# A graph layer on one core: who adds the mask, who finds the row maxima, and who issues which DMA in the edge stage

## The chip, the cores and the metric

The kernel runs on one core of a Trainium2 chip. The metric is the device time of one execution in microseconds (us); the figure before the change is the median of three runs.

## What is computed

The reference has two graph layers behind a layer norm and a ReLU each, with a residual sum. The change touches the second one only:

```python
def _L1_gnn_ref(x, adj, weight, bias, node_w, edge_w):
    node_att = jax.nn.softmax(x @ node_w, axis=0)
    h = x @ edge_w
    e = h @ h.T
    e = jnp.where(adj > 0, e, NEG_BIG)
    edge_att = jax.nn.softmax(e, axis=1)
    combined_att = node_att * edge_att
    support = x @ weight
    output = adj * combined_att @ support
    return output + bias
...
h = jnp.maximum(_layernorm(x, axis=-1), 0.0)
x = x + _L1_gnn_ref(h, adj, ...)
```

There are N = 3327 nodes and 256 features, in f32; `NEG_BIG` is -9e15. The row softmax needs the maximum of each row of the masked 3327 x 3327 scores before the exponential.

## The kernel before

The program has four parts: the first layer (two steps, from the start to about 3400 us of the span), `phase_mid` (layer norm, `h`, `support`), and `phase_edges`, the stage of the change, which runs from 3650 us to the end. `phase_edges` takes the rows in `NT` = 26 blocks of 128. Per block t, in the order in which the data goes:

- SyncE's queue loads 128 rows of the adjacency into `adj` (3 slots, 1664 KB, line 1155 and 1161) and 128 x 256 of the residual into `xr` (2 slots, lines 1157 and 1165). In the loop of lines 1158 to 1165 it waits for `w_ready` of t, loads block t+3, then waits for `out_ready` of t, stores the result of t (line 1163), and loads `xr` of t+2.
- VectorE, `penalty` (line 1210): 0 or NEG_BIG in bf16, `pen`, from `adj`.
- TensorE, `scores` (lines 1289 and 1290): 7 chunks (six of 512 columns, one of 255), in 2 PSUM banks by turns. A chunk takes six f16 matmuls (`hth`, `htl` are the high and low halves of `h`) and a seventh one of `identb` with `pen`, which adds the mask in PSUM. Chunk n waits until chunk n-2 has been taken (`lg_free`), and the first chunk of a block for `pen_ready`.
- VectorE, `take` (line 1218): copies a chunk to `em` (3 slots) and finds its row maxima with the same instruction, into `mx`; `highest` (line 1223) reduces the 7 maxima to `nb`.
- ScalarE, `exponent` (line 1186): exp over the row with its sum.
- GpSimd (line 1180): `em` times `adj`, 128 x 3328 (`w_ready`). It may start only behind the exponential.
- TensorE, `transposes` (line 1299), 26 blocks of 128 columns in 7 groups q; ScalarE copies each group to f16, `wh` (line 1200), and VectorE makes the low half `wl` (line 1265).
- TensorE, `attend` (lines 1310 to 1312): three matmuls of 256 columns for each of the 26.
- VectorE, `finish` (lines 1227 to 1237): reciprocal of the sum, residual plus bias (line 1229), factor times node attention (line 1231), and the output (line 1237), which goes to `o`.

The order on each engine is written out by hand, with scores running two blocks ahead (`AHEAD`). In block t TensorE does, for q = 0 to 6: transposes(t, q), scores(t+2, q), and from q = 2 on attend(t, q-2); then attend(t, 5) and attend(t, 6). VectorE does for each q: wl(t, q), take(t+2, q), and behind q = 2 finish(t-1); then highest(t+2) and penalty(t+3). ScalarE does for each q the copy, and behind q = 1 exponent(t+1). Every engine waits in its own order, so an instruction that waits holds all that stand behind it on its engine.

Of the kernel before, what the change touches and what calls it, by code (L numbers as in the profile page):

```python
# [15 lines left out]
P = 128  # L16
# [1102 lines left out]
def phase_edges(nc, sem_in, psum, sb_in, env):  # L1119
# [5 lines left out]
    with ExitStack() as c:  # L1125
# [5 lines left out]
        identb = sb("e_identb", [P, P], BF16)  # L1131
# [5 lines left out]
        mx = sb("e_mx", [P, 3, NCH], F32)  # L1137
# [7 lines left out]
            "ax_done", "fac_ready", "xr_ready", "out_ready", "zero", "identb", "pen_ready")}  # L1145
# [5 lines left out]
        @block.sync  # L1151
        def _(sp):
            sp.dma_start(bias[:], env["bias"]).then_inc(S["bias_in"], 16)
            for t in range(3):
                sp.dma_start(adj[:, t], adjR[t]).then_inc(adj_in[t], 16)
            for t in range(2):
                sp.dma_start(xr[:, t], x1_d[:, t, :]).then_inc(xr_in[t], 16)
            for t in range(NT):
                if t + 3 < NT:
                    sp.wait_ge(S["w_ready"], t + 1)  # L1160
                    sp.dma_start(adj[:, t % 3], adjR[t + 3]).then_inc(adj_in[t % 3], 16)
                sp.wait_ge(S["out_ready"], t + 1)
                sp.dma_start(out[:, t, :], o[:, t % 2]).then_inc(stored[t % 2], 16)  # L1163
                if t + 2 < NT:
                    sp.dma_start(xr[:, t % 2], x1_d[:, t + 2, :]).then_inc(xr_in[t % 2], 16)  # L1165
            for u in range(2):
                sp.wait_ge(stored[u], 16 * (NT // 2))

        @block.gpsimd
        def _(pool):  # L1170
# [6 lines left out]
            for t in range(NT):  # L1177
                pool.wait_ge(adj_in[t % 3], 16 * (t // 3 + 1))
                pool.wait_ge(S["exp_done"], t + 1)
                nc.gpsimd.tensor_tensor(em[:, t % 3], em[:, t % 3], adj[:, t % 3], ALU.mult).then_inc(S["w_ready"], 1)  # L1180

        @block.scalar
        def _(act):
# [6 lines left out]
            nc.scalar.activation(natt[:], natt[:], ACT.Exp, bias=col[:, 2:3], accum_out=col[:, 3:4]).then_inc(na["exps"], 1)  # L1190
            act.wait_ge(S["zero"], 1)
            exponent(0)
            for t in range(NT):
                for q in range(NGRP):
# [6 lines left out]
                    if q == 1 and t + 1 < NT:  # L1201
                        exponent(t + 1)

        @block.vector
        def _(dve):
            def penalty(t):
                dve.wait_ge(adj_in[t % 3], 16 * (t // 3 + 1))
                if t >= 2:
                    dve.wait_ge(S["lg_done"], NCH * (t - 1))
                nc.vector.tensor_scalar(pen[:, t % 2, 0:N], adj[:, t % 3, 0:N], 0.0, NEG_BIG, ALU.is_le, ALU.mult).then_inc(S["pen_ready"], 1)  # L1210

            def take(t, ch):
                n = NCH * t + ch
                w = chunk_width(ch)
                if ch == 0 and t >= 3:
                    dve.wait_ge(S["tr_done"], NGRP * (t - 2))
                dve.wait_ge(S["lg_done"], n + 1)
                nc.vector.tensor_scalar(em[:, t % 3, ch * CH:ch * CH + w], psL[n % 2][:, 0:w], 1.0, None, ALU.mult, ALU.max,  # L1218
                                        accum_out=mx[:, t % 3, ch:ch + 1]).then_inc(S["lg_free"], 1)

            def highest(t):
                dve.wait_ge(S["lg_free"], NCH * (t + 1))
                nc.vector.tensor_reduce(nb[:, t % 3:t % 3 + 1], mx[:, t % 3], AX.X, ALU.max, negate=True).then_inc(S["nb_ready"], 1)

            def finish(t):
                u = t % 2
                nc.vector.reciprocal(fac[:, u:u + 1], den[:, t % 3:t % 3 + 1]).then_inc(S["fac_ready"], 1)
                dve.wait_ge(xr_in[u], 16 * (t // 2 + 1))
                nc.vector.tensor_tensor(xr[:, u], xr[:, u], bias[:], ALU.add).then_inc(S["xr_ready"], 1)  # L1229
                dve.wait_ge(S["fac_ready"], 2 * t + 1)  # L1230
                nc.vector.tensor_tensor(fac[:, u:u + 1], fac[:, u:u + 1], natt[:, t:t + 1], ALU.mult).then_inc(S["fac_ready"], 1)
# [9 lines left out]
            nc.vector.tensor_copy(identb[:], ident[:]).then_inc(S["identb"], 1)  # L1241
            dve.wait_ge(S["bias_in"], 16)
# [34 lines left out]
        def _(pe):  # L1277
            def scores(t, ch):
# [3 lines left out]
                if ch == 0:  # L1282
                    pe.wait_ge(S["pen_ready"], t + 1)
# [3 lines left out]
                for i, (lhs, rhs) in enumerate(((hth, hth), (hth, htl), (htl, hth))):  # L1287
                    for k in range(KC):
                        nc.tensor.matmul(bank, lhs[:, k, rows], rhs[:, k, cols], start=(i + k == 0), stop=False)  # L1289
                nc.tensor.matmul(bank, identb[:], pen[:, t % 2, cols], start=False, stop=True).then_inc(S["lg_done"], 1)  # L1290
# [25 lines left out]
            pe.wait_ge(S["identb"], 1)  # L1316
# [49 lines left out]
```

## Time and profile before

| what | value |
|---|---|
| median of 3 runs | 4305.14 us (4302.59 to 4307.82) |
| the profiled execution: its time | 4310.23 us |
| the profiled execution: its span | 4308.4 us |
| mean granted TensorE clock over the span | 0.884 |
| PE busy / PEld busy | 3101.3 us (72%) / 2139.9 us (50%) |
| DVE busy | 3669.6 us (85%) |
| ACT busy | 2984.8 us (69%) |
| POOL busy | 321.9 us (7%) |

PE is TensorE's matmul side, PEld its weight loads, DVE is VectorE, ACT is ScalarE, POOL is GpSimd, SP is SyncE, and SPq and ACTq are the sides of SP and ACT that issue DMAs. The busy shares are means over stages with different limits, so they are read here by stage. In a timeline a row gives start, duration, engine, line, operation, and tiles (written <- read), then the count; what stands in brackets is the idle time before it and what ended it. Two matmuls in a row overlap in their durations, so the cost of a group is read from its start to the start of the next.

### The profile page before, as it was taken

The numbers are of one execution on the slowest core, as the hardware profiler recorded it, in microseconds if no ns is written. First come the engines' busy times: TensorE is split into PE (matmuls) and PEld (weight loads), VectorE is DVE, ScalarE is ACT, GpSimd is POOL, SyncE is SP. The second block draws the span as 40 slices with busy tenths as digits, with TensorE's granted clock in tenths as the row PEclk, the third lists the DMA queues.
The fourth block names the chain that finished last, engine by engine and source line by source line (L and its number), as shares of the span: only waits on it lengthen the run. The fifth ranks groups of instructions, "written<-read, shape, count | busy, mean of one in ns | idle before, by whom it ended". The sixth has DMA issues, their size and how long they took to land. (4 is left out here: it accounts for less than half of the span.)

```text
span 4308.4 us, 41843 instructions
## 1 busy us (share of the span) xinstructions
PE 3101.3 (72%) x14280; PEld 2139.9 (50%) x14330; DVE 3669.6 (85%) x4935; ACT 2984.8 (69%) x3947; POOL 321.9 (7%) x319
## 2 busy tenths in 40 slices
PE   2646787877878785558786877968777344988888
PEld 2335565665656664424353443534444233566666
DVE  3399999999999999599999999999999543666766
ACT  1299999999999971499999999899980111222222
POOL 0000000000000000000000000000000132322322
PEclk9968988988989997879898988989888667999999
DMA  0111212212212121311111111111111231122221
GB/s 34 42 52 56 90 49 73 76 63 82 69 61 82 57 81 52 125 33 41 46 32 37 41 36 42 32 37 43 36 43 31 82 97 64 67 91 74 74 92 45
DMA packets 108035, 254.24 MB, mean 59 GB/s; under 512 B 11888, under 2 KB 47792, under 8 KB 104368
## 3 DMA queue, kind: packets, MB, share of 16 engines
q1 hardware_dynamic: 89104, 224.32, 16.2%
q10 hardware_dynamic: 18720, 27.27, 1.7%
q8 instruction: 113, 1.85, 0.2%
q14 instruction: 98, 0.80, 0.1%
HBM read 217.47 MB, written 34.08 MB: 58 GB/s over the span
## 5 line engine op out<-in xcount | busy, mean ns | idle before, releaser
L619 DVE SCALAR_TENSOR_TENSOR s_dump<-s_rows,s_mid 128x3327 bf16<-128x3327 f32 x684 | 2518.1, 3681 | 0.7 <-issue 0.2
L569 ACT ACTIVATE s_adump<-s_rows,s_mid 128x3327 bf16<-128x3327 f32 (+1 forms) x304 | 933.6, 3071 | 9.9
L574 ACT ACTIVATE s_adump<-s_rows,s_mid 128x3327 bf16<-128x3327 f32 (+1 forms) x304 | 930.0, 3059 | 5.9 <-ACT s_sx_out L480 3.1
L767 PE MATMUL bank<-x,s_slab 128*128 128x512 f32 x1352 | 615.5, 608 | 0.0
L810 PE MATMUL bank<-hb,s_wT 128*128 128x256 f32 x1352 | 359.8, 411 | 121.1 <-ACT s_wT L458 120.9
L810 PE MATMUL bank<-xab,s_wT 128*128 128x256 f32 x1352 | 351.2, 404 | 114.9 <-ACT s_wT L458 114.9
L767 PEld LDWEIGHTS bank<-x,s_slab 128*128 128x128 f32 x1352 | 265.4, 197 | 314.9 <-issue 308.8
L1200 ACT ACTIVATE e_wh<-bank 128x512 f16<-128x512 f32 (+1 forms) x182 | 102.5, 565 | 448.2 <-PE bank L1299 448.1
L458 ACT ACTIVATE s_wT<-bank 128x512 f32<-128x512 f32 (+1 forms) x364 | 201.2, 553 | 287.5 <-PE bank L799 287.5
L799 PE MATMUL bank<-ident,s_rows 128*128 128x128 f32 x1352 | 227.7, 295 | 181.0 <-DVE s_rows L639 181.0
L746 PE MATMUL bank<-kh,qs 128*128 128x512 f16 (+1 forms) x364 | 145.4, 399 | 282.2 <-DVE s_rows L598 271.7
L810 PEld LDWEIGHTS bank<-hb,s_wT 128*128 128x128 f32 x1352 | 260.0, 203 | 171.8 <-ACT s_wT L458 81.5
L810 PEld LDWEIGHTS bank<-xab,s_wT 128*128 128x128 f32 x1352 | 257.6, 201 | 166.8 <-ACT s_wT L458 74.2
L767 PE MATMUL bank<-hb,s_slab 128*128 128x257 f32 x1352 | 340.2, 406 | 0.0
L799 PEld LDWEIGHTS bank<-ident,s_rows 128*128 128x128 f32 x1352 | 186.2, 156 | 244.8 <-DVE s_rows L639 189.2
L767 PEld LDWEIGHTS bank<-hb,s_slab 128*128 128x128 f32 x1352 | 278.8, 207 | 53.9 <-issue 4.8
L598 DVE TENSOR_SCALAR_CACHE_REDUCE s_rows<-bank 128x512 f32<-128x512 f32 (+1 forms) x364 | 233.1, 644 | 61.3 <-PE bank L747 59.2
L1180 POOL TENSOR_TENSOR e_rows<-e_rows,e_adj 128x3328 f32<-128x3328 f32 x26 | 187.9, 7226 | 429.1 <-ACT e_rows L1186 429.1
L746 PEld LDWEIGHTS bank<-kh,qs 128*128 128x128 f16 x364 | 38.1, 105 | 356.2 <-DVE s_rows L598 321.0
L1265 DVE TENSOR_TENSOR e_wl<-bank,e_wh 128x512 f16<-128x512 f32 (+1 forms) x182 | 117.8, 649 | 106.1 <-ACT e_wh L1200 106.1
L639 DVE SCALAR_TENSOR_TENSOR s_rows<-s_rows,s_mid 128x3327 f32<-128x3327 f32 x52 | 191.4, 3680 | 0.9
L1310 PE MATMUL bank<-sup,e_wh 128*128 128x256 f16 x676 | 185.1, 274 | 8.7 <-DVE e_wl L1265 7.4
(175 smaller groups left out, 4657.1 us busy)
## 6 DMA issues: line engine op xcount, KB each, us to landing
s_slab<-adjT_dram SPq DMA_DIRECT2D x104, 448.0 KB, 3.8
e_adj<-adjR_dram SPq DMA_DIRECT2D x26, 1664.0 KB, 7.4
s_slab<-adjT_dram SPq DMA_DIRECT2D x104, 384.0 KB, 3.6
strip<-adjR_dram SPq DMA_DIRECT2D x52, 448.0 KB, 3.5
strip<-adjR_dram SPq DMA_DIRECT2D x52, 384.0 KB, 3.3
su_d<-s_su_out ACTq DMA_DIRECT2D x26, 256.0 KB, 2.0
zu_d<-s_zu_out ACTq DMA_DIRECT2D x26, 256.0 KB, 2.0
sx_d<-s_sx_out ACTq DMA_DIRECT2D x26, 256.0 KB, 2.0
```

The lines of the kernel that those rows point to most:

```text
L458: nc.scalar.activation(wT[:, n % 2, 0:w], bank_of("quad", n)[:, 0:w], ACT.Copy).then_inc(S["ev_done"], 1)
L569: nc.scalar.activation(adump[:], row(g, 2), ACT.Sign, bias=st(mid, g, 2), accum_out=cnt[:]).then_inc(S["a_eval"], 1)
L574: nc.scalar.activation(adump[:], row(g, 2), ACT.Relu, bias=st(mid, g, 2), accum_out=gap[:]).then_inc(S["a_eval"], 1)
L598: nc.vector.tensor_scalar(rows[:, home(g, r), ch * CH:ch * CH + w], psL[n % 2][:, 0:w], 1.0, None, ALU.mult, ALU.max, accum_out=mx[:, home ...
L619: nc.vector.scalar_tensor_tensor(out=dump[:], in0=row(g, r), scalar=st(mid, g, r), in1=row(g, r), op0=ALU.is_gt, op1=ALU.mult, accum_out=s ...
L639: nc.vector.scalar_tensor_tensor(out=row(g, r), in0=row(g, r), scalar=st(mid, g, r), in1=row(g, r), op0=ALU.is_gt, op1=ALU.mult, accum_out ...
L746: nc.tensor.matmul(psL[n % 2][:, 0:w], lhs, kh2[:, cols], start=True, stop=False)
L767: ins = nc.tensor.matmul(acc, slab[:, i % NSLAB, j - PIECES[p], :], s_op[:, j, 0:SN], start=False, stop=(j == NT - 1))
L799: ins = nc.tensor.transpose(bank[:, k * P:(k + 1) * P], rows[:, home(g, r), j * P:(j + 1) * P], ident[:])
L810: ins = nc.tensor.matmul(psA[f % 2][:, 0:D], wT[:, n % 2, k * P:(k + 1) * P], a_op[:, j, 0:D], start=(j == 0), stop=(j == NT - 1))
L1180: nc.gpsimd.tensor_tensor(em[:, t % 3], em[:, t % 3], adj[:, t % 3], ALU.mult).then_inc(S["w_ready"], 1)
L1310: nc.tensor.matmul(acc, wh[:, n % 4, blk], sup[:, j, 0:D], start=(j == 0), stop=False)
```

## The change

The mask leaves TensorE: the seventh matmul of each chunk, with `identb`, is gone, and so is TensorE's wait for `pen_ready`. `take` becomes a sum of the bank and `pen` on VectorE without the maxima, and `highest` reduces the whole row of 3327 from `em`. The sum of residual and bias goes from VectorE's `finish` to GpSimd, behind the multiplication of the same block. Line 1231 becomes an instruction with a per-partition scalar in place of one with two tensors. The store of the result and the next load of `xr` go from SyncE's queue to ScalarE's, behind the copy q = 4 of the next block; SyncE keeps the adjacency loads, which now wait for `w_ready` alone. `penalty` waits for the takes of the block that used its slot.

```diff
--- before.py
+++ after.py
@@ -1128,13 +1128,11 @@
         em = sb("e_rows", [P, 3, NPAD], F32)
         adj = sb("e_adj", [P, 3, NPAD], F32)
         pen = sb("e_pen", [P, 2, NPAD], BF16)
-        identb = sb("e_identb", [P, P], BF16)
         wh = sb("e_wh", [P, 4, CH], F16)
         wl = sb("e_wl", [P, 4, CH], F16)
         xr = sb("e_xr", [P, 2, D], F32)
         bias = sb("e_bias", [P, D], F32)
         o = sb("e_out", [P, 2, D], F32)
-        mx = sb("e_mx", [P, 3, NCH], F32)
         nb, den = (sb("e_" + n, [P, 3], F32) for n in ("nb", "den"))
         fac = sb("e_fac", [P, 2], F32)
         natt = sb("e_natt", [P, NT], F32)
@@ -1142,7 +1140,7 @@
         na = {n: sem("e_node_" + n) for n in ("cut", "top", "all_top", "shift", "exps", "total", "inverse", "done")}
         S = {n: sem("e_" + n) for n in (
             "bias_in", "lg_done", "lg_free", "nb_ready", "exp_done", "w_ready", "tr_done", "hi_done", "lo_done",
-            "ax_done", "fac_ready", "xr_ready", "out_ready", "zero", "identb", "pen_ready")}
+            "ax_done", "fac_ready", "xr_ready", "out_ready", "zero", "pen_ready")}
         adj_in = [sem(f"e_adj_in{i}") for i in range(3)]
         xr_in, stored = ([sem(f"e_{n}{i}") for i in range(2)] for n in ("xr_in", "stored"))
         c.callback(cleared)
@@ -1155,16 +1153,9 @@
                 sp.dma_start(adj[:, t], adjR[t]).then_inc(adj_in[t], 16)
             for t in range(2):
                 sp.dma_start(xr[:, t], x1_d[:, t, :]).then_inc(xr_in[t], 16)
-            for t in range(NT):
-                if t + 3 < NT:
-                    sp.wait_ge(S["w_ready"], t + 1)
-                    sp.dma_start(adj[:, t % 3], adjR[t + 3]).then_inc(adj_in[t % 3], 16)
-                sp.wait_ge(S["out_ready"], t + 1)
-                sp.dma_start(out[:, t, :], o[:, t % 2]).then_inc(stored[t % 2], 16)
-                if t + 2 < NT:
-                    sp.dma_start(xr[:, t % 2], x1_d[:, t + 2, :]).then_inc(xr_in[t % 2], 16)
-            for u in range(2):
-                sp.wait_ge(stored[u], 16 * (NT // 2))
+            for t in range(NT - 3):
+                sp.wait_ge(S["w_ready"], t + 1)
+                sp.dma_start(adj[:, t % 3], adjR[t + 3]).then_inc(adj_in[t % 3], 16)
 
         @block.gpsimd
         def _(pool):
@@ -1178,6 +1169,10 @@
                 pool.wait_ge(adj_in[t % 3], 16 * (t // 3 + 1))
                 pool.wait_ge(S["exp_done"], t + 1)
                 nc.gpsimd.tensor_tensor(em[:, t % 3], em[:, t % 3], adj[:, t % 3], ALU.mult).then_inc(S["w_ready"], 1)
+                if t == 0:
+                    pool.wait_ge(S["bias_in"], 16)
+                pool.wait_ge(xr_in[t % 2], 16 * (t // 2 + 1))
+                nc.gpsimd.tensor_tensor(xr[:, t % 2], xr[:, t % 2], bias[:], ALU.add).then_inc(S["xr_ready"], 1)
 
         @block.scalar
         def _(act):
@@ -1188,6 +1183,12 @@
 
             act.wait_ge(na["shift"], 1)
             nc.scalar.activation(natt[:], natt[:], ACT.Exp, bias=col[:, 2:3], accum_out=col[:, 3:4]).then_inc(na["exps"], 1)
+            def store(t):
+                act.wait_ge(S["out_ready"], t + 1)
+                act.dma_start(out[:, t, :], o[:, t % 2]).then_inc(stored[t % 2], 16)
+                if t + 2 < NT:
+                    act.dma_start(xr[:, t % 2], x1_d[:, t + 2, :]).then_inc(xr_in[t % 2], 16)
+
             act.wait_ge(S["zero"], 1)
             exponent(0)
             for t in range(NT):
@@ -1200,13 +1201,18 @@
                     nc.scalar.activation(wh[:, n % 4, 0:w], psT[n % 4][:, 0:w], ACT.Copy).then_inc(S["hi_done"], 1)
                     if q == 1 and t + 1 < NT:
                         exponent(t + 1)
+                    if q == 4 and t >= 1:
+                        store(t - 1)
+            store(NT - 1)
+            for u in range(2):
+                act.wait_ge(stored[u], 16 * (NT // 2))
 
         @block.vector
         def _(dve):
             def penalty(t):
                 dve.wait_ge(adj_in[t % 3], 16 * (t // 3 + 1))
                 if t >= 2:
-                    dve.wait_ge(S["lg_done"], NCH * (t - 1))
+                    dve.wait_ge(S["lg_free"], NCH * (t - 1))
                 nc.vector.tensor_scalar(pen[:, t % 2, 0:N], adj[:, t % 3, 0:N], 0.0, NEG_BIG, ALU.is_le, ALU.mult).then_inc(S["pen_ready"], 1)
 
             def take(t, ch):
@@ -1215,20 +1221,20 @@
                 if ch == 0 and t >= 3:
                     dve.wait_ge(S["tr_done"], NGRP * (t - 2))
                 dve.wait_ge(S["lg_done"], n + 1)
-                nc.vector.tensor_scalar(em[:, t % 3, ch * CH:ch * CH + w], psL[n % 2][:, 0:w], 1.0, None, ALU.mult, ALU.max,
-                                        accum_out=mx[:, t % 3, ch:ch + 1]).then_inc(S["lg_free"], 1)
+                if ch == 0:
+                    dve.wait_ge(S["pen_ready"], t + 1)
+                cols = slice(ch * CH, ch * CH + w)
+                nc.vector.tensor_tensor(em[:, t % 3, cols], psL[n % 2][:, 0:w], pen[:, t % 2, cols], ALU.add).then_inc(S["lg_free"], 1)
 
             def highest(t):
                 dve.wait_ge(S["lg_free"], NCH * (t + 1))
-                nc.vector.tensor_reduce(nb[:, t % 3:t % 3 + 1], mx[:, t % 3], AX.X, ALU.max, negate=True).then_inc(S["nb_ready"], 1)
+                nc.vector.tensor_reduce(nb[:, t % 3:t % 3 + 1], em[:, t % 3, 0:N], AX.X, ALU.max, negate=True).then_inc(S["nb_ready"], 1)
 
             def finish(t):
                 u = t % 2
                 nc.vector.reciprocal(fac[:, u:u + 1], den[:, t % 3:t % 3 + 1]).then_inc(S["fac_ready"], 1)
-                dve.wait_ge(xr_in[u], 16 * (t // 2 + 1))
-                nc.vector.tensor_tensor(xr[:, u], xr[:, u], bias[:], ALU.add).then_inc(S["xr_ready"], 1)
                 dve.wait_ge(S["fac_ready"], 2 * t + 1)
-                nc.vector.tensor_tensor(fac[:, u:u + 1], fac[:, u:u + 1], natt[:, t:t + 1], ALU.mult).then_inc(S["fac_ready"], 1)
+                nc.vector.tensor_scalar(fac[:, u:u + 1], fac[:, u:u + 1], natt[:, t:t + 1], None, ALU.mult).then_inc(S["fac_ready"], 1)
                 if t >= 2:
                     dve.wait_ge(stored[u], 16 * (t // 2))
                 dve.wait_ge(S["ax_done"], NGRP * (t + 1))
@@ -1238,8 +1244,6 @@
                                                op0=ALU.mult, op1=ALU.add).then_inc(S["out_ready"], 1)
 
             nc.vector.memset(em[:, :, N:NPAD], 0.0).then_inc(S["zero"], 1)
-            nc.vector.tensor_copy(identb[:], ident[:]).then_inc(S["identb"], 1)
-            dve.wait_ge(S["bias_in"], 16)
             dve.wait_ge(na["cut"], 1)
             nc.vector.tensor_reduce(col[:, 0:1], natt[:], AX.X, ALU.max).then_inc(na["top"], 1)
             for t in range(AHEAD):
@@ -1279,15 +1283,13 @@
                 n = NCH * t + ch
                 w = chunk_width(ch)
                 rows, cols = slice(t * P, (t + 1) * P), slice(ch * CH, ch * CH + w)
-                if ch == 0:
-                    pe.wait_ge(S["pen_ready"], t + 1)
                 if n >= 2:
                     pe.wait_ge(S["lg_free"], n - 1)
                 bank = psL[n % 2][:, 0:w]
                 for i, (lhs, rhs) in enumerate(((hth, hth), (hth, htl), (htl, hth))):
                     for k in range(KC):
-                        nc.tensor.matmul(bank, lhs[:, k, rows], rhs[:, k, cols], start=(i + k == 0), stop=False)
-                nc.tensor.matmul(bank, identb[:], pen[:, t % 2, cols], start=False, stop=True).then_inc(S["lg_done"], 1)
+                        ins = nc.tensor.matmul(bank, lhs[:, k, rows], rhs[:, k, cols], start=(i + k == 0), stop=(i + k == 3))
+                ins.then_inc(S["lg_done"], 1)
 
             def transposes(t, q):
                 n = NGRP * t + q
@@ -1313,7 +1315,6 @@
                 ins.then_inc(S["ax_done"], 1)
 
             pe.wait_ge(S["zero"], 1)
-            pe.wait_ge(S["identb"], 1)
             for t in range(AHEAD):
                 for ch in range(NCH):
                     scores(t, ch)
```

## Rows read from the trace of the kernel before

**Rows 1.** The page's chain that ended last, by line, share of the span.

```profile
DMA e_adj<-adjR_dram 4%; DVE e_xr L1229 3%; PE bank L1289 1%; ACT e_rows L1186 1%; DVE e_pen L1210 1%; PE bank L1299 1%; DVE e_wl L1265 0%; DVE e_rows L1218 0%; ACT e_wh L1200 0%; DVE e_out L1237 0%; PE bank L1310 0%; SPq L1165 0%; PE bank L1311 0%; PE bank L1312 0%; SPq L1163 0%
```

**Rows 2.** Chain inside one block: start us, duration us, what.

```profile
3942.87 8.14 DMA e_adj<-adjR_dram
...
3969.39 7.79 DMA e_adj<-adjR_dram
```

**Rows 3.** Timeline of POOL (start, duration, engine, line): multiplies of t=2 and t=24.

```profile
3710.91 7.22 POOL L1180 TENSOR_TENSOR e_rows<-e_rows,e_adj 128x3328 f32<-128x3328 f32 x1 [13.95 <-ACT e_rows L1186]
...
4253.50 7.22 POOL L1180 TENSOR_TENSOR e_rows<-e_rows,e_adj 128x3328 f32<-128x3328 f32 x1 [16.90 <-ACT e_rows L1186]
```

**Rows 4.** Waits of PE, 3683 to 4270 us: total us, times, longest us.

```profile
PE bank L1289 <- DVE e_rows L1218: 36.2, 23, 1.6
...
PE bank L1289 <- DVE e_pen L1210: 29.4, 22, 2.5
```

**Rows 5.** Timeline of PE in block 0, full clock, and the start of block 1.

```profile
3683.31 0.66 PE L1299 MATMUL bank<-ident,e_rows 128*128 128x128 f32 x4 [1.23 <-POOL e_rows L1180]
...
3687.26 0.60 PE L1299 MATMUL bank<-ident,e_rows 128*128 128x128 f32 x4
...
3687.69 0.59 PE L1289 MATMUL bank<-hth 128*128 128x512 f16 x2
...
3688.99 0.38 PE L1290 MATMUL bank<-e_pen,e_identb 128*128 128x512 bf16 x1
...
3689.20 0.27 PE L1310 MATMUL bank<-sup,e_wh 128*128 128x256 f16 x1
...
3690.51 0.60 PE L1299 MATMUL bank<-ident,e_rows 128*128 128x128 f32 x4
...
3704.55 0.60 PE L1299 MATMUL bank<-ident,e_rows 128*128 128x128 f32 x4
```

**Rows 6.** Timeline of all engines, 3731 to 3746 us, block 2.

```profile
3731.81 0.60 PE L1299 MATMUL bank<-ident,e_rows 128*128 128x128 f32 x4
...
3736.24 7.22 POOL L1180 TENSOR_TENSOR e_rows<-e_rows,e_adj 128x3328 f32<-128x3328 f32 x1 [18.10 <-ACT e_rows L1186]
...
3736.61 0.69 DVE L1265 TENSOR_TENSOR e_wl<-bank,e_wh 128x512 f16<-128x512 f32 x1 [1.95 <-ACT e_wh L1200]
...
3737.90 5.84 DVE L1229 TENSOR_TENSOR e_xr<-e_xr,e_bias 128x256 f32<-128x256 f32 x1
...
3744.90 0.68 DVE L1218 TENSOR_SCALAR_CACHE_REDUCE e_rows<-bank 128x512 f32<-128x512 f32 x1
```

**Rows 7.** Instructions of one line: duration ns min/median/max, first and last start, forms.

```profile
L1229 DVE TENSOR_TENSOR e_xr<-e_xr,e_bias x26: 406/5844/6428, 3712.6 to 4300.7; 128x256 f32<-128x256 f32 x26
...
L1210 DVE TENSOR_SCALAR e_pen<-e_adj x26: 1895/1896/1897, 3658.3 to 4245.6; 128x3327 bf16<-128x3327 f32 x26
...
L112 DVE TENSOR_REDUCE mean<-xs x1: 7027/7027/7027, 13.6 to 13.6; 128x26 f32<-128x6656 f32 x1
```

**Rows 8.** Timelines of DVE and POOL, 3676 to 3684 us.

```profile
3676.03 7.22 POOL L1180 TENSOR_TENSOR e_rows<-e_rows,e_adj 128x3328 f32<-128x3328 f32 x1 [10.79 <-ACT e_rows L1186]
...
3682.84 0.45 DVE L1258 TENSOR_SCALAR e_natt<-e_natt,e_col 128x26 f32<-128x26 f32 x1
```

**Rows 9.** Groups by line, 3300 to 4308 us; one ACT queue issue from the timeline.

```profile
L957 POOL TENSOR_TENSOR m_tin<-m_tin,m_bet 128x256 f32<-128x256 f32 x26 | 20.0, 768 | 2.1 <-DMA m_bet<-beta_dram 2.1
...
2019.43 0.33 ACTq L470 DMA_DIRECT2D xa_d<-s_xa_out  x1
```

**Rows 10.** Timeline of PE, 3845 to 3860 us.

```profile
3853.67 0.60 PE L1289 MATMUL bank<-hth 128*128 128x512 f16 x2 [2.50 <-DVE e_pen L1210]
...
3855.72 1.06 PE L1299 MATMUL bank<-ident,e_rows 128*128 128x128 f32 x4 [0.22 <-issue]
```

**Rows 11.** Timeline of PE: first transposes of blocks 24 and 25.

```profile
4270.11 1.47 PE L1299 MATMUL bank<-ident,e_rows 128*128 128x128 f32 x12
...
4290.77 1.47 PE L1299 MATMUL bank<-ident,e_rows 128*128 128x128 f32 x12
```

## The prediction

> **What bounds the kernel now.** I read the chain that ended last first. Over the whole span most of it is the first layer, which the change leaves alone; in the edges it names the adjacency load and line 1229 [rows 1]. Inside one block it is a cycle [rows 2]: an adjacency load lands after 8.14 us, then come `penalty`, the first scores chunk, transposes, copies, the exponential, line 1229, the output, and the next load is issued 26.5 us after the last. SyncE's queue explains it: the load of block t+4 stands behind the wait for the output of block t, though its slot was free one block earlier.
>
> The period is (4253.50 - 3710.91) / 22 = 24.66 us per block [rows 3]. TensorE's work in it, from starts at full clock [rows 5]: four transposes 0.43 (3687.26 to 3687.69), a chunk without the mask 1.30 (to 3688.99), the mask matmul 0.21 (to 3689.20), four blocks of `attend` 1.31 (to 3690.51). A block has 6.5 of each (3327 columns are 6.5 chunks, 26 blocks are 6.5 groups): 6.5 x (0.43 + 1.30 + 0.21 + 1.31) = 21.1. Block 0, with hardly a wait, took 3704.55 - 3683.31 = 21.2, which agrees. The rest is two waits [rows 4]: 36.2 / 23 = 1.6 for `take` and 29.4 / 22 = 1.3 for `penalty`; 21.1 + 1.6 + 1.3 = 24.0. The missing 0.6 I put down to a few blocks in which the clock fell behind a long wait (2.50 us, then four transposes at 1.06 in place of 0.60, half clock) [rows 10].
>
> Where does the wait for `take` come from? Line 1229 adds two SBUF tensors of 256 columns. It takes 0.41 us alone and 5.84 as a rule [rows 7], because it starts beside GpSimd's multiplication and ends at that one's end: 3736.24 + 7.22 = 3743.46, and 3737.90 + 5.84 = 3743.74 [rows 6]. Line 1265, with one operand in PSUM and one in SBUF, runs its usual 0.69 in the same stretch [rows 6]. So VectorE stands for 5.4 us, and TensorE's sixth chunk of the block misses its bank.
>
> **Part by part, per block.**
> - Mask matmul: TensorE loses 6.5 x 0.21 = 1.4 us and comes to 6.5 x 3.04 = 19.8. On the path, as TensorE is the busiest engine of the block.
> - Adjacency loads behind `w_ready` alone: issued some 20 us sooner. The wait for `penalty`, 1.3 us, goes, and so do the long waits and the clock's falls: 0.6.
> - `take` becomes a sum of PSUM and SBUF. Not in the trace for bf16 and f32 output; the nearest row is line 1265, 0.69 against 0.68 for the old form [rows 6]. Bounds: 0.68, and twice that if bf16 were slow; I take 0.69. It loses its accumulator read of 0.08 (the page of the profile shows DVE with slack here), so nothing on balance.
> - `highest` over 3327 columns in place of 7: line 112 reduces 6656 in 7.03 us, so 3.5 us [rows 7]. Is it hidden? Behind the last chunk TensorE has `attend` 4, 5, 6: 1.31 + 1.31 + 0.66 = 3.3 us. VectorE needs 0.7 (`take`) + 3.6 + 1.8 (`penalty`, 1.90 with the overlap [rows 7]) = 6.1, so it is 2.9 us late in the next block. Then wl 0.6 and `take` 0.7: the third chunk may start at 4.2; TensorE would reach it at 2 x 1.73 + 0.43 = 3.9. So 0.3 us of it shows, and the rest hides behind `attend` and two chunks.
> - Residual plus bias on GpSimd: about 0.77 [rows 9] behind the multiplication. GpSimd is idle for two thirds of the block, and `finish` reads the sum a block later. Nothing. Its wait for `xr` stands ahead of the next multiplication; `xr` is issued at about 11 us of the block and lands in some 2 us, the next multiplication starts over 10 us later.
> - Store and `xr` load on ScalarE: two issues of about 0.33 to 0.43 [rows 9], behind copy q = 4 and ahead of copy q = 5, which TensorE makes ready only 3 us later. Hidden. The wait for `out_ready` there holds copy 5; it is short as long as `finish` is done by about 14 us of the block.
> - Line 1231 becomes a TENSOR_SCALAR with a per-partition scalar, both sides in SBUF. This is the step that decides. Now it runs after GpSimd is done; with line 1229 gone it comes in the middle of the multiplication. The nearest row is line 1258, the same form with 26 columns: 0.45 us, where one column takes 0.15 in line 1231's old form, and it ended at 3682.84 + 0.45 = 3683.29, GpSimd's multiplication at 3676.03 + 7.22 = 3683.25 [rows 8]. It seems to have waited. For one column no row tells; line 1210, with an odd count, runs at twice the pace of line 112 per element [rows 7], so an odd count does not keep this form from its fast mode. Bounds: 0.15 us, and a wait to GpSimd's end. I take the wait, since the nearest row has it.
>
> The Trainium skill (SBUF — State Buffer, "Who interferes with whom") has it that `tensor_scalar` can enter the modes that use the port pair shared with GpSimd and then blocks fully, and that `tensor_reduce` never does on trn2. Its Vector Engine (DVE) Microarchitecture Reference, section 5.1, gives the two-port mode to counts that are even, or odd and equal on both sides; taken literally one column qualifies. That speaks against this change. The row of 26 columns agrees; no row here shows one column.
>
> With that wait, from the block's first transposes: transposes 1 start at 1.73. In block 2 GpSimd started 4.43 and ended 11.65 behind them, and `take` of chunk 3 ended at 3744.90 + 0.68 - 3731.81 = 13.77 [rows 6]. Less 0.2, as line 1231 gets through by itself at GpSimd's end, plus 0.07 to TensorE: chunk 5 starts at 1.73 + 13.64 = 15.4, where TensorE would be there at 2 x 1.73 + 3 x 3.04 + 0.43 = 13.0. The wait is 2.35 us (and swallows the 0.3): period 19.77 + 2.35 = 22.1 us.
>
> **The sum**, against the profiled span. Start: two row passes stand in series before there is overlap. The first chunk can't be taken sooner (`penalty` waits for the load), `highest` of row 0 adds 3.35, and TensorE, idle meanwhile, redoes a chunk at half clock, about 0.6: block 0 starts at 3683.3 + 4.0 = 3687.3. In it `highest` of row 1 delays the third chunk by some 1.2: 21.0 us, to 3708.3. Blocks 1 to 23: 23 x 22.12 = 508.8, to 4217.1. Block 24 took 4290.77 - 4270.11 = 20.7 [rows 11] and is held by the same stall: 20.5. Block 25 and the end, 4308.4 - 4290.8 = 17.6, stay. 4255.2, which is 53.2 less than 4308.4. The profiled execution took 4310.2, 5.1 over the median, so I take the difference from the median: 4305.1 - 53.2 = 4252 us.
>
> **The rivals.**
> - N, line 1231 doesn't wait. For it: the reciprocal of one column beside it, and no row for one column. Then nothing holds VectorE in mid-block, the period is 19.77 + 0.3 = 20.1 us, and block 24 shortens to the exponential and multiplication, about 12.6. 3708.3 + 23 x 20.07 + 12.6 + 17.6 = 4200, 108 less: 4197 us.
> - T, the new `take` waits for GpSimd too, since it now reads `pen`. Against it: line 1265 in the same stretch. Chunk 4 would start at 14.1 in place of 10.0: period 23.9, 12 less in all: 4293 us.
> - C, slower. TensorE's one wait of 2.35 us per block is near the 2.50 behind which the clock fell [rows 10]. If it falls in each block for about 3 us of work, that costs 1.5 us per block, 4287; it needs 53.2 / 23 = 2.3 us per block, 4.6 us at 1.2 GHz, to eat the gain. With two falls, 3.0 us: 4252 + 69 = 4321 us. Against it: waits of 1.6 in every block now, and the clock fell in few blocks.
> - D, the change doesn't do what it says: the loads are still late because another wait stands before them. Each load now waits only for GpSimd's end, which is at 13.4 us of a block, and is needed at the next block's end, some 28 us later for a transfer of 8. Its chance is in that of no change below.
>
> **How the numbers follow.** Forecast 0.56 (4252, own range 4240 to 4268), N 0.30 (4197, 4188 to 4206), T 0.05 and partly so, C 0.05, no change 0.04 (gains given back by something not listed). The two large cases lie on one side, so the range takes both: 4188 to 4275; what is outside is T, C, no change and errors of the sum. A measurement of this kernel can tell about 0.2%, 9 us, from no change: faster 0.91, within 0.04, slower 0.05.
>
> **What would show it.** In the profile after: no line of `identb`; no wait of `penalty` for the load; the reduction of 3327 columns at 3.5 us; TensorE's wait for the new `take` at 2.3 us once per block, with line 1231's successor at some 5 us beside GpSimd's multiplication (forecast), or at 0.15 with waits of 0.3 (N); the sum of PSUM and `pen` at 0.69 (against T); granted clock 1.00 from block 1 to 23 (against C). Periods between GpSimd's multiplications of 22.1 or 20.1 us. I am wrong if VectorE's lateness at the block's border, 2.9 us, is much larger: at 3.5 us more, `exponent` would wait for `nb` too, and everything behind it.

## The result, and the profile after

The kernel after takes 4202.0 us (median of 4 runs, 4199.0 to 4205.0), the kernel before 4304.0 us in the same runs: ratio 0.976, interval 0.9745 to 0.9779. The forecast was 4252 us with a range of 4188 to 4275, and rival N, in which line 1231 does not wait, had 4197 us. So the gain is 102 us where the forecast had 53: the time came out where the rival had it.

The page of the kernel after, its span and busy times (share of the span, instructions):

```profile
span 4202.4 us, 41322 instructions
...
PE 3075.0 (73%) x14148; PEld 2134.0 (51%) x14148; DVE 3617.7 (86%) x4726; ACT 2984.6 (71%) x3947; POOL 332.6 (8%) x345
```

What TensorE waits for in the edges from block 0 on, 3683 to 4203 us (total us, times, longest us), where [rows 4] had 36.2 and 29.4 us:

```profile
PE bank L1291 <- DVE e_rows L1227: 1.9, 1, 1.9
PE bank L1312 <- DVE e_wl L1269: 1.5, 3, 0.6
```

The 1.9 us are in block 0, the 1.5 us in the last two blocks. In between the hold shows on the side of the weight loads alone (the same view for PEld, 3717 to 4158 us):

```profile
PEld bank L1291 <- DVE e_rows L1227: 7.0, 22, 0.3
```

That is 0.3 us in each of 22 blocks. The period is read from GpSimd's timeline, the first row of which is its first instruction of the edges, the others the multiplications of t = 2 and t = 24:

```profile
3653.05 0.21 POOL L1162 TENSOR_SCALAR_AFFINE_SELECT e_natt<-natt_in 128x26 f32<-128x26 f32 x1 [15.24 <-POOLq L91]
...
3717.46 7.24 POOL L1171 TENSOR_TENSOR e_rows<-e_rows,e_adj 128x3328 f32<-128x3328 f32 x1 [12.51 <-ACT e_rows L1181]
...
4158.19 7.24 POOL L1171 TENSOR_TENSOR e_rows<-e_rows,e_adj 128x3328 f32<-128x3328 f32 x1 [12.12 <-ACT e_rows L1181]
```

(4158.19 - 3717.46) / 22 = 20.03 us, where [rows 3] gave 24.66. One block border and the middle of block 3, from the timeline of all engines:

```profile
3748.40 0.41 DVE L1227 TENSOR_TENSOR e_rows<-bank,e_pen 128x255 f32<-128x255 f32 x1
...
3748.85 3.62 DVE L1231 TENSOR_REDUCE e_nb<-e_rows 128x1 f32<-128x3327 f32 x1
...
3751.37 0.60 PE L1301 MATMUL bank<-ident,e_rows 128*128 128x128 f32 x4
...
3752.39 1.89 DVE L1216 TENSOR_SCALAR e_pen<-e_adj 128x3327 bf16<-128x3327 f32 x1
...
3754.18 0.68 DVE L1269 TENSOR_TENSOR e_wl<-bank,e_wh 128x512 f16<-128x512 f32 x1
...
3755.52 0.60 PE L1291 MATMUL bank<-hth 128*128 128x512 f16 x2
...
3757.53 7.24 POOL L1171 TENSOR_TENSOR e_rows<-e_rows,e_adj 128x3328 f32<-128x3328 f32 x1 [12.12 <-ACT e_rows L1181]
...
3758.52 0.68 DVE L1227 TENSOR_TENSOR e_rows<-bank,e_pen 128x512 f32<-128x512 f32 x1
...
3759.30 0.21 DVE L1237 TENSOR_SCALAR e_fac<-e_fac,e_natt 128x1 f32<-128x1 f32 x1
...
3759.72 0.48 DVE L1243 SCALAR_TENSOR_TENSOR e_out<-bank,e_fac,e_xr 128x256 f32<-128x256 f32 x1 [0.20 <-DVE e_fac L1237]
```

Here is the case that I had set at 0.30. GpSimd multiplies from 3757.53 to 3764.77. Line 1237, the factor, starts at 3759.30 and takes 0.21 us; the output line 1243 follows at 3759.72 and takes 0.48. Neither waits, and the factor's line takes 0.212 to 0.214 us in all its 26 places, 24 of them beside a multiplication. In [rows 6] VectorE stood still from 3737.90 to 3743.74 at this place.

The top rows show the border. The last `take` at 3748.40, the row pass of 3.62 us, `penalty`; wl of the new block begins at 3754.18, TensorE's block at 3751.37: VectorE is 2.8 us late. The third chunk starts at 3755.52, and TensorE would have been there at 3751.37 + 2 x 1.73 + 0.44 = 3755.27. So 0.25 us of the lateness shows.

The groups of the lines that the change made, by shape (count, busy, mean ns, then the idle time before and what ended it), and the stage's busy time and clock from block 1 to block 23:

```profile
L1227 DVE TENSOR_TENSOR e_rows<-bank,e_pen 128x512 f32<-128x512 f32 x156 | 106.6, 684 | 9.8 <-PE bank L1291 9.8
...
L1231 DVE TENSOR_REDUCE e_nb<-e_rows 128x1 f32<-128x3327 f32 x26 | 94.1, 3619 | 0.9
...
L1175 POOL TENSOR_TENSOR e_xr<-e_xr,e_bias 128x256 f32<-128x256 f32 x26 | 18.9, 728 | 2.0 <-DMA e_xr<-x_d 1.9
...
L1237 DVE TENSOR_SCALAR e_fac<-e_fac,e_natt 128x1 f32<-128x1 f32 x26 | 5.6, 214 | 0.9
```

```profile
3717.00:4158.00 441.00, 439.20 (x3217) 321.24 (x3215) 319.69 (x418) 152.16 (x201) 174.35 (x44) 1.00 0.27 95
```

In the second fence the columns are the stretch, its length, the busy times of PE, PEld, DVE, ACT and POOL, the granted clock, the DMA share and GB/s. The clock is 1.00 throughout, so TensorE ran at 2.4 GHz. TensorE's first transposes of blocks 24 and 25:

```profile
4172.07 1.47 PE L1301 MATMUL bank<-ident,e_rows 128*128 128x128 f32 x12
...
4184.67 1.47 PE L1301 MATMUL bank<-ident,e_rows 128*128 128x128 f32 x12
```

### The profile page after: what moved, and what is told of

It reads as the page before. It is cut to its first block and busy times, and to the rows that moved or that the text cites. A ratio compares the mean times of both kernels' runs of the same rounds, so it can differ in the third digit from the quotient of the medians.

```text
span 4202.4 us, 41322 instructions
## 1 busy us (share of the span) xinstructions
PE 3075.0 (73%) x14148; PEld 2134.0 (51%) x14148; DVE 3617.7 (86%) x4726; ACT 2984.6 (71%) x3947; POOL 332.6 (8%) x345
## 5 line engine op out<-in xcount | busy, mean ns | idle before, releaser
L767 PE MATMUL bank<-hb,s_slab 128*128 128x257 f32 x1352 | 357.0, 421 | 0.0
L767 PEld LDWEIGHTS bank<-hb,s_slab 128*128 128x128 f32 x1352 | 291.3, 217 | 59.9 <-issue 6.4
```

The source lines that it names most:

```text
L767: ins = nc.tensor.matmul(acc, slab[:, i % NSLAB, j - PIECES[p], :], s_op[:, j, 0:SN], start=False, stop=(j == NT - 1))
```

## Which parts of the change made the gain

**e1, the queues alone** on the kernel before.

```diff
-                sp.wait_ge(S["out_ready"], t + 1)
-                sp.dma_start(out[:, t, :], o[:, t % 2]).then_inc(stored[t % 2], 16)
-                if t + 2 < NT:
-                    sp.dma_start(xr[:, t % 2], x1_d[:, t + 2, :]).then_inc(xr_in[t % 2], 16)
...
+                    if q == 4 and t >= 1:
+                        store(t - 1)
```

> The kernel before with one part of the change: ScalarE's queue stores the results and loads the residual, SyncE's queue has the adjacency loads alone. Theory (two separate holds per block: the late load, 1.3 us and 0.6 us of lowered clock, and the VectorE stall of line 1229, 1.6 us): the wait for the penalty goes, the wait for take stays at 1.6 us, period about 22.8 us, 4304 - 23 x 1.9 = 4261 us. Rival (the load is late only because the stall makes the output late, so the queue order is worth nothing or everything): 4304 us or 4225 us.

Measured 4274.5 us against 4308.4 us of before in its runs, ratio 0.992 (0.990 to 0.994). The two multiplications of t = 2 and t = 24, and TensorE's one wait that is left in these blocks:

```profile
3713.16 7.22 POOL L1173 TENSOR_TENSOR e_rows<-e_rows,e_adj 128x3328 f32<-128x3328 f32 x1 [13.95 <-ACT e_rows L1179]
...
4218.49 7.22 POOL L1173 TENSOR_TENSOR e_rows<-e_rows,e_adj 128x3328 f32<-128x3328 f32 x1 [15.75 <-ACT e_rows L1179]
```

```profile
PE bank L1293 <- DVE e_rows L1222: 37.1, 23, 1.6
```

Period (4218.49 - 3713.16) / 22 = 22.97 us. The wait for `penalty` is gone, the wait for `take` stays at 37.1 / 23 = 1.6 us, as the theory of two holds had it. The gain is 34 us where it expected 43: it took 1.9 us per block, and the periods give 24.66 - 22.97 = 1.7. From GpSimd's first instruction of the edges to the end, the profiled executions are 37.6 us apart (658.0 and 620.4), as 22 x 1.7 has it.

The busy times and the clock over these 22 blocks, and over the block of the long wait of [rows 10] in the kernel before (columns as above):

```profile
3713.00:4218.00 505.00, 467.18 (x3322) 335.75 (x3364) 371.81 (x594) 151.58 (x198) 158.97 (x22) 1.00 0.24 83
...
3853.00:3878.00 25.00, 22.94 (x151) 15.94 (x153) 16.36 (x28) 6.44 (x9) 7.24 (x1) 0.93 0.23 80
```

In e1 the clock did not fall. In the kernel before it fell to 1.2 GHz for a short while in three of the 22 blocks, behind waits of 2.50, 2.05 and 2.23 us.

**e2, the addition on GpSimd and the factor's new form** on the kernel before. Both are in it, so it does not tell them apart; e4 below shows what the form is worth.

```diff
+                pool.wait_ge(xr_in[t % 2], 16 * (t // 2 + 1))
+                nc.gpsimd.tensor_tensor(xr[:, t % 2], xr[:, t % 2], bias[:], ALU.add).then_inc(S["xr_ready"], 1)
...
-                nc.vector.tensor_tensor(xr[:, u], xr[:, u], bias[:], ALU.add).then_inc(S["xr_ready"], 1)
...
-                nc.vector.tensor_tensor(fac[:, u:u + 1], fac[:, u:u + 1], natt[:, t:t + 1], ALU.mult).then_inc(S["fac_ready"], 1)
+                nc.vector.tensor_scalar(fac[:, u:u + 1], fac[:, u:u + 1], natt[:, t:t + 1], None, ALU.mult).then_inc(S["fac_ready"], 1)
```

> The kernel before with another part alone: residual plus bias on GpSimd and the factor with a per-partition scalar; queues, mask matmul and maxima as before. Theory: VectorE's stall goes, the output comes 5.6 us sooner, and the load behind it on SyncE's queue too, which is more than the 2.6 us that VectorE waits for it on average. So both waits go: period 21.2 us, block 24 8 us shorter, 4304 - 23 x 3.5 - 8 = 4216 us. Rival (two separate holds): only the 1.6 us per block and block 24, about 4304 - 37 - 8 = 4259 us.

Measured 4225.9 us, ratio 0.981 (0.979 to 0.983). The same two rows of GpSimd's timeline:

```profile
3713.24 7.24 POOL L1180 TENSOR_TENSOR e_rows<-e_rows,e_adj 128x3328 f32<-128x3328 f32 x1 [13.26 <-ACT e_rows L1190]
...
4179.26 7.23 POOL L1180 TENSOR_TENSOR e_rows<-e_rows,e_adj 128x3328 f32<-128x3328 f32 x1 [13.27 <-ACT e_rows L1190]
```

Period (4179.26 - 3713.24) / 22 = 21.18 us: TensorE's own 21.1 with the mask matmul. Both waits are gone though the queues are as they were. The result comes sooner by the stall, and the load that stands behind it on SyncE's queue with it: VectorE, which waited 53.5 us in 22 blocks for adjacency loads in the kernel before, waits for none here.

**e3, both, and the mask still on TensorE** (the edits of e1 and e2 in one kernel; the lines below are a part of them).

```diff
-                sp.wait_ge(S["out_ready"], t + 1)
-                sp.dma_start(out[:, t, :], o[:, t % 2]).then_inc(stored[t % 2], 16)
...
+                nc.gpsimd.tensor_tensor(xr[:, t % 2], xr[:, t % 2], bias[:], ALU.add).then_inc(S["xr_ready"], 1)
...
+                    if q == 4 and t >= 1:
+                        store(t - 1)
```

> The kernel before with both of these parts, mask matmul on TensorE and maxima taken with the copy as before. Theory: TensorE bounds the block at 21.2 us, as in e2, so the queues add nothing to it: 4216 us; what is left to the kernel after (4202 us) is the mask's part, 23 x 1.1 us less 4 us at the start and less 1 us in block 0, about 20 us, rather more than is missing. Rival (the mask's part is nothing, since VectorE's row pass costs what the matmul gives back): 4202 us.

Measured 4224.8 us, ratio 0.980 (0.979 to 0.982). GpSimd's timeline, its first instruction of the edges and the same two multiplications:

```profile
3654.35 0.27 POOL L1164 TENSOR_SCALAR_AFFINE_SELECT e_natt<-natt_in 128x26 f32<-128x26 f32 x1 [15.25 <-POOLq L91]
...
3714.66 7.24 POOL L1173 TENSOR_TENSOR e_rows<-e_rows,e_adj 128x3328 f32<-128x3328 f32 x1 [13.27 <-ACT e_rows L1183]
...
4180.68 7.23 POOL L1173 TENSOR_TENSOR e_rows<-e_rows,e_adj 128x3328 f32<-128x3328 f32 x1 [13.19 <-ACT e_rows L1183]
```

Again 21.18 us. Given the addition on GpSimd, the queues are worth nothing that can be told (4225.9 and 4224.8). So of the 102 us some 80 come from taking away VectorE's stall. The step from here to the kernel after, 4202.0 us, is the mask's: 22 x (21.18 - 20.03) = 25 us won, and 4 us given back at the start. There GpSimd's multiplication of t = 2 began 3714.66 - 3654.35 = 60.3 us behind the first instruction of GpSimd in the edges, in the kernel after 3717.46 - 3653.05 = 64.4. (e3 and the kernel after were not timed together; their edge stages alone, 571.6 and 549.4 us, are 22 us apart as well.) The mask's step is the matmul, the sum in `take` and the row pass together; no run takes them apart.

**e5, the queues of before put back** into the kernel after.

```diff
+                sp.wait_ge(S["out_ready"], t + 1)
+                sp.dma_start(out[:, t, :], o[:, t % 2]).then_inc(stored[t % 2], 16)
+                if t + 2 < NT:
+                    sp.dma_start(xr[:, t % 2], x1_d[:, t + 2, :]).then_inc(xr_in[t % 2], 16)
...
-                    if q == 4 and t >= 1:
-                        store(t - 1)
```

> The kernel after with the queues of before: SyncE's queue stores, loads the residual, and has the adjacency load behind the output. Theory: the output now comes at about 8 us of a block, the load lands at about 16 us, the penalty needs it at about 22 us, so it is hidden: 4202 us, no wait of the penalty for the load. Rival (the queues are a part of the gain by themselves): the penalty waits again, 1.3 us per block, 4232 us.

Measured 4204.7 us, ratio 0.977 (0.975 to 0.978), where the kernel after in the same runs (e7) had 4202.7, ratio 0.976. GpSimd's multiplications of t = 2 and t = 24 in e5:

```profile
3719.81 7.24 POOL L1178 TENSOR_TENSOR e_rows<-e_rows,e_adj 128x3328 f32<-128x3328 f32 x1 [12.52 <-ACT e_rows L1188]
...
4160.56 7.24 POOL L1178 TENSOR_TENSOR e_rows<-e_rows,e_adj 128x3328 f32<-128x3328 f32 x1 [12.10 <-ACT e_rows L1188]
```

Period 20.03 us, as with the change, and the medians are 1.9 us apart, within the intervals. From this side too the queues' part of the gain is too small to be told from nothing.

> The kernel after itself, as the measure for e5 and e8: 4202 us.

e7, the kernel after itself, had 4202.7 us (4199.0 to 4203.5).

## Does the factor's instruction wait for GpSimd?

**e4, line 1237 with two tensors** again, all else as after.

```diff
-                nc.vector.tensor_scalar(fac[:, u:u + 1], fac[:, u:u + 1], natt[:, t:t + 1], None, ALU.mult).then_inc(S["fac_ready"], 1)
+                nc.vector.tensor_tensor(fac[:, u:u + 1], fac[:, u:u + 1], natt[:, t:t + 1], ALU.mult).then_inc(S["fac_ready"], 1)
```

> The kernel after with line 1237 back in its old form, two tensors of one column in SBUF. It is the case on which the forecast stood: VectorE held in mid-block until GpSimd's multiplication ends. Theory (two SBUF tensors wait for GpSimd whatever their size): the line takes about 5 us beside the multiplication, TensorE waits 2.3 us per block for the fourth take, period 22.1 us, 4252 us; the granted clock stays at 1.00. Rival 1 (an instruction of one column never waits): 4202 us. Rival 2 (the clock falls behind each such wait): 4287 us or more.

Measured 4260.8 us, ratio 0.989 (0.988 to 0.991). The multiplications of t = 2 and t = 24:

```profile
3716.16 7.22 POOL L1171 TENSOR_TENSOR e_rows<-e_rows,e_adj 128x3328 f32<-128x3328 f32 x1 [12.51 <-ACT e_rows L1181]
...
4204.14 7.22 POOL L1171 TENSOR_TENSOR e_rows<-e_rows,e_adj 128x3328 f32<-128x3328 f32 x1 [10.70 <-ACT e_rows L1181]
```

The factor's line in e4, durations in ns (min/median/max); TensorE's waits for `take`; busy times and clock over the one long period:

```profile
L1237 DVE TENSOR_TENSOR e_fac<-e_fac,e_natt x26: 159/5472/6050, 3717.9 to 4250.3; 128x1 f32<-128x1 f32 x26
```

```profile
PE bank L1291 <- DVE e_rows L1227: 43.6, 23, 2.2
```

```profile
3804.00:3828.00 24.00, 21.68 (x148) 15.01 (x146) 19.55 (x19) 6.78 (x10) 7.96 (x2) 0.93 0.24 84
```

One column of two SBUF tensors takes 5.47 us as a rule, beside GpSimd, and 0.16 at the least. Period (4204.14 - 3716.16) / 22 = 22.18 us, with one wait of TensorE per block, 43.6 / 23 = 1.9 us in the mean and 2.2 at most. The two-tensor line is not the form of the forecast, but the hold has the same place and length. So the price that the forecast put on the hold was right: 22.18 - 19.77 = 2.4 us per block, where it had 2.35; it only belongs to another instruction. The clock column (0.93) is rival C: behind one of these waits (2.24 us) the clock fell, and that period was 24.1 us in place of 22.1. It happened once in 22 blocks, not in each.

The time is 9 us over the forecast's 4252. The edge stage of the profiled execution, 4258.1 - 3651.07 = 607.0 us, is 51.0 shorter than before, where the forecast had 53.2; the fall of the clock is 2 of the difference. The rest comes in with the step from the profiled execution to the median, on which more below.

**e6, the factor's instruction over 1, 2, 3, 4, 7 or 26 columns** by turns. Only the first column is used.

```diff
+                wd = (1, 2, 3, 4, 7, 26)[t % 6]
...
-                nc.vector.tensor_scalar(fac[:, u:u + 1], fac[:, u:u + 1], natt[:, t:t + 1], None, ALU.mult).then_inc(S["fac_ready"], 1)
+                nc.vector.tensor_scalar(fac[:, u, 0:wd], fac[:, u, 0:wd], natt[:, t:t + 1], None, ALU.mult).then_inc(S["fac_ready"], 1)
```

> The kernel after with line 1237 over 1, 2, 3, 4, 7 or 26 columns by turns, block by block (only the first column is used). All but the last two stand beside GpSimd's multiplication. Theory (the instruction waits for GpSimd where it runs in its fast mode, which one column does not enter): one column 0.21 us, 2, 4 and 26 columns about 4 to 5 us; 3 and 7 columns as well, since line 1216 with 3327 columns is fast. Rival 1 (odd counts that small do not wait): 3 and 7 at 0.22 us. Rival 2 (the form with a per-partition scalar never waits, and line 1258 before was slow for another reason): all at 0.21 to 0.25 us.

Measured 4251.1 us in one run; it is there for its trace. The groups of the factor's line by shape (count, busy us, mean ns, idle before):

```profile
L1239 DVE TENSOR_SCALAR e_fac<-e_fac,e_natt 128x26 f32<-128x26 f32 x4 | 22.5, 5634 | 0.1
L1239 DVE TENSOR_SCALAR e_fac<-e_fac,e_natt 128x2 f32<-128x2 f32 x5 | 22.2, 4431 | 0.2
L1239 DVE TENSOR_SCALAR e_fac<-e_fac,e_natt 128x7 f32<-128x7 f32 x4 | 21.9, 5484 | 0.1
L1239 DVE TENSOR_SCALAR e_fac<-e_fac,e_natt 128x3 f32<-128x3 f32 x4 | 21.9, 5481 | 0.1
L1239 DVE TENSOR_SCALAR e_fac<-e_fac,e_natt 128x4 f32<-128x4 f32 x4 | 21.9, 5478 | 0.1
L1239 DVE TENSOR_SCALAR e_fac<-e_fac,e_natt 128x1 f32<-128x1 f32 x5 | 1.1, 215 | 0.2
```

Two blocks in the timeline of VectorE and GpSimd, one with 2 columns and one with 1:

```profile
3739.05 5.48 DVE L1239 TENSOR_SCALAR e_fac<-e_fac,e_natt 128x2 f32<-128x2 f32 x1
...
3849.84 0.21 DVE L1239 TENSOR_SCALAR e_fac<-e_fac,e_natt 128x1 f32<-128x1 f32 x1
...
3737.28 7.23 POOL L1172 TENSOR_TENSOR e_rows<-e_rows,e_adj 128x3328 f32<-128x3328 f32 x1 [12.11 <-ACT e_rows L1182]
...
3848.07 7.24 POOL L1172 TENSOR_TENSOR e_rows<-e_rows,e_adj 128x3328 f32<-128x3328 f32 x1 [6.66 <-ACT e_rows L1182]
```

It is the count, and the step is between one and two. One column takes 0.215 us on the mean of its five places. Four of them lie beside a multiplication, 3849.84 among them, with GpSimd busy from 3848.07 to 3855.31. Two columns, begun at 3739.05, end at 3744.53, as GpSimd does at 3744.51. Three and seven wait like two and four, so an odd count does not help. (The mean of 4.43 us for two columns has among its five places the last block's, where GpSimd was idle and the line took 0.23 us.) GpSimd's multiplications follow each other at 22.1 us as a rule where the wait was, at 20.0 where it was not.

## Two further steps

**e8, penalty sooner**: from the end of the block to behind q = 5.

```diff
+                    if q == 5 and t + AHEAD + 1 < NT:
+                        penalty(t + AHEAD + 1)
...
-                if t + AHEAD + 1 < NT:
-                    penalty(t + AHEAD + 1)
```

> The kernel after with penalty moved from the end of a block to behind q = 5, before the last take and the row pass. Theory (TensorE's only hold left is VectorE's lateness of 2.9 us at the border, which shows as 0.3 us at the third chunk): VectorE is 1.1 us late instead, the wait goes, period 19.8 us, 6 us less: 4196 us. Rival (penalty holds the last take, and the exponential behind the row pass): no change or some us more.

Measured 4198.1 us (4196.1 to 4199.9), ratio 0.975 (0.974 to 0.976); the interval overlaps that of e7. VectorE's timeline at a border, and GpSimd's multiplications of t = 2 and t = 24:

```profile
3825.01 1.89 DVE L1216 TENSOR_SCALAR e_pen<-e_adj 128x3327 bf16<-128x3327 f32 x1
...
3827.59 3.62 DVE L1231 TENSOR_REDUCE e_nb<-e_rows 128x1 f32<-128x3327 f32 x1
...
3717.14 7.25 POOL L1171 TENSOR_TENSOR e_rows<-e_rows,e_adj 128x3328 f32<-128x3328 f32 x1 [12.51 <-ACT e_rows L1181]
...
4152.27 7.24 POOL L1171 TENSOR_TENSOR e_rows<-e_rows,e_adj 128x3328 f32<-128x3328 f32 x1 [11.85 <-ACT e_rows L1181]
```

Period (4152.27 - 3717.14) / 22 = 19.78 us, TensorE's work of 19.77 with no wait beside it. `penalty` (3825.01) now runs ahead of the row pass (3827.59), and nothing but the pass makes VectorE late. 22 x 0.25 = 5.5 us; the medians differ by 4.6.

**e9, maxima chunk by chunk in the first two row blocks**, on top of e8.

```diff
+                if t < AHEAD:
+                    dve.wait_ge(S["lg_free"], n + 1)
+                    nc.vector.tensor_reduce(mx[:, t, ch:ch + 1], em[:, t % 3, cols], AX.X, ALU.max).then_inc(mx_ready, 1)
```

> The kernel of e8, and in the first two blocks of rows the maxima are found chunk by chunk, a small reduction behind each take, in place of one pass over the row. Theory (the row pass costs 4 us at the start, where nothing hides it: GpSimd's multiplication of t = 2 came 64.4 us behind the stage's start in the kernel after and 60.5 before): a reduction of 512 columns is about 0.6 us and goes into VectorE's idle time between two takes, 0.6 to 2.2 us, so the start is about 4 us shorter and the median 4194 us. Rival (take and reduction together are over the 1.3 us in which TensorE makes a chunk, and the lead is spent): within 1 us of e8, 4198 us.

Measured 4192.3 us (4191.6 to 4193.6), ratio 0.974 (0.9725 to 0.9751), the lowest of all. VectorE's timeline in the first row block, GpSimd's first instruction of the edges and its multiplication of t = 2:

```profile
3668.59 0.68 DVE L1229 TENSOR_TENSOR e_rows<-bank,e_pen 128x512 f32<-128x512 f32 x1
...
3669.91 0.68 DVE L1229 TENSOR_TENSOR e_rows<-bank,e_pen 128x512 f32<-128x512 f32 x1
...
3649.34 0.21 POOL L1164 TENSOR_SCALAR_AFFINE_SELECT e_natt<-natt_in 128x26 f32<-128x26 f32 x1 [15.26 <-POOLq L91]
...
3710.58 7.24 POOL L1173 TENSOR_TENSOR e_rows<-e_rows,e_adj 128x3328 f32<-128x3328 f32 x1 [11.85 <-ACT e_rows L1183]
```

`take` and reduction together go at 1.32 us a chunk (3668.59 to 3669.91), as fast as TensorE makes one (1.30). GpSimd's multiplication of t = 2 comes 3710.58 - 3649.34 = 61.2 us behind the stage's start, 3.2 sooner than in e8, of the 4 that the row pass had cost. TensorE waited 2.1 us ahead of block 0 here, and its clock fell: the first four transposes took 1.12 us where the next took 0.60. That may be a part of what is missing. The medians of e8 and e9 differ by 5.8 us, and the edge stages, which are all that differs in the code, by 543.6 - 540.5 = 3.1; so about half of the 5.8 is not the change's.

## Why the prediction was right or wrong, step by step

- What bounds the kernel. Right: two waits of TensorE per block and a lowered clock now and then. But the 0.6 us per block that it put down to the clock is too much for it: three falls, each 0.93 over 25 us, cost 3 x 0.07 x 25 = 5 us, 0.24 per block. e1 had no fall, and 22.97 - 21.18 - 1.6 still leaves 0.2. What the rest is was not shown. What it said of the load on SyncE's queue was true of the chain, but the load was no hold of its own. e2 took away the stall of line 1229 alone and both waits went. The prediction booked 1.3 + 0.6 us to the queue; e1 shows them with the stall in place (34 us), e2, e3 and e5 that they come to nothing without it.
- Mask matmul, 1.4 us of TensorE's time. Right: 21.18 in e2 and e3, 20.03 and 19.78 behind it.
- `take` as a sum with bf16, taken at 0.69. Right: 0.684, also beside GpSimd (3758.52), which ends rival T.
- `highest`, 3.5 us, lateness 2.9 (its own terms, 6.1 - 3.3, give 2.8), of which 0.3 shows. Right: 3.62, 2.8 and 0.25. That VectorE took on a pass of 3.6 us per block and TensorE felt 0.25 of it is the part that the change could most easily have lost on.
- Addition on GpSimd and DMAs on ScalarE at nothing. Right: 0.73 us, and in the kernel after ScalarE's two issues run beside its idle time. Rival D is out as well: from 3720 us on VectorE waits for no load.
- Line 1231. This step failed, and with it the forecast: it put a wait of 2.35 us per block on this line, and the line did not wait (0.21 us beside GpSimd). "I take the wait, since the nearest row has it": the row had 26 columns, and e6 puts the step between 1 and 2. The row itself was read rightly: line 1258's 0.45 us held a wait, since the same instruction takes 0.24 us in the kernel after, at 3693.80, where GpSimd is idle. The Trainium skill (Vector Engine (DVE) Microarchitecture Reference, section 5.1) lets even counts, or odd and equal ones, into the two-port mode, and its page SBUF — State Buffer, "Who interferes with whom", lets that mode wait for GpSimd. For 2, 3, 4, 7 and 26 columns the runs agree. One column took 0.215 us in e6, and the measurement decides. The rule is worded for a dimension that is not of size one, so the prediction's "taken literally one column qualifies" read more into it than it says. The same "Who interferes with whom" has an instruction with two SBUF inputs contend with a GpSimd instruction that reads SBUF; the runs agree down to one column (5.47 us in e4).
- The sum of the start. Counted from GpSimd's first instruction of the edges, block 0 began 3.5 us later than before, where 4.0 was expected, and took 21.9 us, where 21.0 was (its third chunk waited 1.9 us and not 1.2): 0.4 us too low in all. Block 24 in rival N: 12.6 expected, 4184.67 - 4172.07 = 12.6 measured. The whole edge stage, from GpSimd's first instruction to the end, went from 4308.4 - 3650.45 (its first instruction before) = 658.0 to 4202.4 - 3653.05 = 549.4 us: 108.6 less, and N said 108. The span changed by 106.0, since the parts before the edges, which the change leaves alone, took 2.6 us longer in this execution. The medians are 102.0 us apart, 6 less than N's 108. The prediction took its difference against one profiled execution, which was 5.1 us over the median, and subtracted it from the median; that is likely where the 5 us between 4197 and 4202 come from. Which part of the median execution is the shorter one isn't shown, as only one execution of the kernel before has a trace.
- The slower case. The clock fell once in e4, where each block had the wait it was to follow, and not once between blocks 1 and 23 of the kernel after. As a mechanism it was there, its size far from the 2.3 us per block that it needed.

The range held the result only because it took in N, to which the prediction gave 0.30 against 0.56 for its own case. The point forecast had half of the gain, because of a wait that was not there; that the range fits is the merit of the rival and, for the forecast, luck. The rows before could not settle the weight between the two cases, since none of them has this form with one column beside GpSimd. What told them apart afterwards was one column against two.

## What to carry to other kernels

When VectorE and GpSimd work beside each other, ask of each small VectorE instruction whether it needs what they share: one such wait of 5 us in mid-block cost this kernel more (82 us in e2) than the whole mask on TensorE (22), directly and through the load that stood behind its result. Moving one such instruction away can bring the next one into its place: with the old form of the factor in the kernel after (e4), 58 us come back. Before a second hold in the same loop is given a price of its own, ask whether it would still be there with the first one gone. And a pass over a row on an engine that is late at a border costs only what is left of it when the bound engine reaches the first buffer that depends on it, except at the start, where nothing hides it.

## What the runs showed of the hardware

- A TENSOR_SCALAR with a per-partition scalar, SBUF to SBUF in f32, waits for the end of GpSimd's SBUF instruction with 2, 3, 4, 7 or 26 columns (5.48 us) and does not with one (0.215 us). A TENSOR_TENSOR of two SBUF tensors waits with one column too (5.47 us).
- An instruction of VectorE with one operand in PSUM and one in SBUF doesn't wait: 0.68 us for the sum with `pen`, 0.48 us for the output line, both beside GpSimd.
- TensorE's granted clock fell to its lower level behind waits of 2.05 to 2.50 us, but not behind each: in three of 22 blocks of the kernel before, and in one of 22 in e4, where a wait of 1.9 us in the mean (2.24 at most) came every 22 us. It did not fall in the 22 blocks of e1, whose waits were 1.6 us.
